# Queries' and keys' parts kept in four slots each, and a head's loads issued as eight transfers of 24 rows

## The reference

```
x = x + attn0(layernorm(x))     # 16 heads of 8 features, causal, with a bias by relative position, then Wo
x = x + ffn0(layernorm(x))      # three tree-routed feed-forward nets give q, k, v of one wide attention
x = x + attn1(layernorm(x))     # 16 heads of 8 features; softmax over all keys, causal mask afterwards
x = x + ffn1(layernorm(x))      # gated, mixed with the token before

# attn0, for a head:                          # attn1, for a head:
sim = q @ k.T + bias;  sim[j > i] = -inf      alpha = softmax(q @ k.T / sqrt(8));  alpha[j > i] = 0
out = softmax(sim) @ v                        out = alpha @ v
```

## Time and profile before

| what | value |
|---|---|
| median of 3 runs | 1780.42 us (1780.28 to 1783.19) |
| the profiled execution | 1783.86 us, of which the span is 1782.1 us |
| open (attn0's projection) | 0 to 65.5 us |
| heads1 (attn0's 64 heads) | 65.5 to about 500 us |
| trees and wide attention | about 500 to 1000 us |
| proj3 (attn1's projection) | about 1000 to 1043 us |
| heads3 (attn1's 64 heads) | 1043 to about 1720 us |
| busy over the span | PE 91%, DVE 85%, ACT 72%, POOL 46% |
| DMA over the span | 141.89 MB, of which loads of heads 512 x 96 KB |

### The profile page before, as it was taken

The page is one execution under the profiler, slowest core; times in us unless marked ns, Lnnn a source line. Parts: engine busy times, 40 slices in busy tenths (PEclk is TensorE's granted clock), DMA queues, the critical chain, the costliest instruction groups (busy, mean ns, idle before and its releaser), DMA issues. The chain is left out here.

```text
span 1782.1 us, 47495 instructions
## 1 busy us (share of the span) xinstructions
PE 1613.3 (91%) x18834; PEld 1038.2 (58%) x18858; DVE 1518.7 (85%) x2248; ACT 1276.2 (72%) x2523; POOL 817.8 (46%) x1533
## 2 busy tenths in 40 slices
PE   5599999999976999999899549999999999999966
PEld 3376667666665887877688314444444444444544
DVE  8699999999856999988677768999999999999735
ACT  6488878888834444454565628888989898998955
POOL 5488888888845001000340323444444444444446
PEclk9699999999965999999999868999999999999978
DMA  7522222323172766565000351111121121112031
GB/s 247 207 85 86 87 90 87 98 86 98 52 148 45 97 95 91 93 90 69 0 1 1 144 184 47 56 56 55 59 65 59 52 73 51 60 53 71 26 76 48
DMA packets 119910, 141.89 MB, mean 80 GB/s; under 512 B 22221, under 2 KB 80778, under 8 KB 119690
## 3 DMA queue, kind: packets, MB, share of 16 engines
q1 hardware_dynamic: 119258, 138.79, 30.8%
q10 hardware_dynamic: 432, 0.07, 0.0%
HBM read 92.70 MB, written 44.98 MB: 77 GB/s over the span
## 5 line engine op out<-in xcount | busy, mean ns | idle before, releaser
L888 DVE TENSOR_REDUCE heads_mx<-heads_psM 128x1 f32<-128x1024 f32 x512 | 602.1, 1219 | 48.4 <-PE heads_psM L979 32.2
L959 ACT ACTIVATE heads_probs<-heads_psS 128x512 f32<-128x512 f32 x1024 | 546.1, 601 | 77.7 <-PE heads_psS L1002 71.7
L928 POOL TENSOR_TENSOR heads_masked<-heads_probs,g_tri 128x128 f32<-128x128 f32 x512 | 233.7, 456 | 360.8 <-ACT heads_probs L959 360.7
L654 POOL TENSOR_TENSOR heads_probs<-heads_probs,one_ebias 128x256 f32<-128x256 f32 (+1 forms) x512 | 341.6, 689 | 76.8 <-ACT heads_probs L686 76.1
L615 DVE TENSOR_REDUCE heads_mx<-heads_psM 128x1 f32<-128x1024 f32 (+7 forms) x512 | 348.8, 748 | 23.7 <-PE heads_psM L697 23.0
L686 ACT ACTIVATE heads_probs<-heads_psS 128x512 f32<-128x512 f32 x576 | 316.3, 603 | 67.6 <-PE heads_psS L697 62.4
L979 PE MATMUL heads_psM<-three_kS,three_qS 48*128 48x512 bf16 x1024 | 230.4, 395 | 20.5 <-PEq L2050 11.6
L1002 PE MATMUL heads_psS<-three_qS,three_kS 50*128 50x512 bf16 x1024 | 238.0, 389 | 0.7 <-ACT heads_probs L959 0.3
L1510 ACT ACTIVATE trees_hid_hi<-trees_hid 128x512 fp32r<-128x512 f32 x192 | 121.6, 633 | 152.4 <-DVE trees_hid L1531 151.5
L1531 DVE SCALAR_TENSOR_TENSOR trees_hid<-trees_psH,g_b,trees_chosen 128x512 f32<-128x512 f32 x192 | 143.8, 749 | 31.8 <-DMA trees_chosen<-leaf_choice 15.1
L1027 PE MATMUL heads_psO<-heads_probs,heads_ones_only 128*32 128x128 f32 x1920 | 162.0, 284 | 0.0
(11 more groups left out here) (273 smaller groups left out, 3174.3 us busy)
## 6 DMA issues: line engine op xcount, KB each, us to landing
trees_chosen<-leaf_choice SPq DMA_DIRECT2D x96, 256.0 KB, 7.6
head_outputs<-g_small SPq DMA_DIRECT2D x128, 128.0 KB
one_qS<-q_parts SPq DMA_DIRECT2D x128, 96.0 KB
one_kS<-k_parts SPq DMA_DIRECT2D x128, 96.0 KB
three_qS<-q_parts SPq DMA_DIRECT2D x128, 96.0 KB
three_kS<-k_parts SPq DMA_DIRECT2D x128, 96.0 KB
q_parts<-g_w SPq DMA_DIRECT2D x8, 768.0 KB, 4.6
k_parts<-g_w SPq DMA_DIRECT2D x8, 768.0 KB, 5.8
```

Source lines behind the costliest of these rows:

```text
L654: pool.tensor_tensor(pr[:, a:a + w], pr[:, a:a + w], bass.AP(eb.tensor, eb.offset + NEAR - 1, [list(eb.ap[0]), [-1, w]]), ALU.mult).then_i ...
L888: dve.tensor_reduce(mx[:, n % 2, k:k + 1], psM[k % 2][:, :], AXX, ALU.max, negate=True).then_inc(max_taken, 1)
L928: pool.tensor_tensor(masked[n % 2][:, kb, :], probs[n % 2][:, kb, kb * P:(kb + 1) * P], g["tri"][:, 0:P], ALU.mult).then_inc(near_done, 1)
L959: act.activation(probs[n % 2][:, kb, h * CH:(h + 1) * CH], ring.bank(i)[:, :], ACT.Exp).then_inc(slot_taken, 1)
```

## The change

The parts are kept in DRAM in four slots, not six (`KEPT`): for queries high, high, middle, low; for keys low, middle, high, high. A tile's 48 rows are now two runs of three neighbouring slots: q takes slots 0 to 2 and then 1 to 3 (high, high, middle, then high, middle, low), k takes 1 to 3 and then 0 to 2 (middle, high, high, then low, middle, high). These are the same six products in another order. Each run is a transfer of its own, of 24 rows, so `Handed.load` issues eight transfers for a head, all on the same semaphore, and what waits for them waits for 128 counts. A store of the high part writes two slots, the others one, so a batch is 8 x 128 rows, 2 MB.

```diff
+KEPT = PARTS + 1
+Q_KEPT = [(0, 2), (2, 1), (3, 1)]
+K_KEPT = [(2, 2), (1, 1), (0, 1)]
...
-                at = b * (PAIRS * P * T)
-                for i, (dst, (start, step, count)) in enumerate(((g["q_dram"], Q_PAIRS[part]), (g["k_dram"], K_PAIRS[part]))):
+                at = b * (KEPT * P * T)
+                for i, (dst, (start, count)) in enumerate(((g["q_dram"], Q_KEPT[part]), (g["k_dram"], K_KEPT[part]))):
                     src = hand.parts[u][:, i, part, :]
-                    sp.dma_start(bass.AP(dst.tensor, at + start * P * T, [[T, P], [step * P * T, count], [1, T]]),
+                    sp.dma_start(bass.AP(dst.tensor, at + start * P * T, [[T, P], [P * T, count], [1, T]]),
                                  bass.AP(src.tensor, src.offset, [list(src.ap[0]), [0, count], [1, T]])).then_inc(stored[u], 16)
...
-        at = (n // HEADS) * PAIRS * P * T + (n % HEADS) * HD * T
-        for tile, src in ((self.qS[u], self.g["q_dram"]), (self.kS[u], self.g["k_dram"])):
+        at = (n // HEADS) * KEPT * P * T + (n % HEADS) * HD * T
+        for tile, src, first in ((self.qS[u], self.g["q_dram"], (0, 1)), (self.kS[u], self.g["k_dram"], (1, 0))):
             for r in (0, HALF):
-                sp.dma_start(tile[r:r + PROWS, :], bass.AP(src.tensor, at, [[P * T, PAIRS], [T, HD], [1, T]])).then_inc(self.loaded[u], 16)
+                for i in range(2):
+                    sp.dma_start(tile[r + i * PARTS * HD:r + (i + 1) * PARTS * HD, :],
+                                 bass.AP(src.tensor, at + first[i] * P * T, [[P * T, PARTS], [T, HD], [1, T]])).then_inc(self.loaded[u], 16)
...
-                    pe.wait_ge(s_loaded[u], (n // BUFS + 1) * 64)
+                    pe.wait_ge(s_loaded[u], (n // BUFS + 1) * 128)
```

More of the change, by code:

```diff
@@ L63 @@
 ROWS = "rows"
-Q_PAIRS = [(0, 1, 3), (3, 1, 2), (5, 1, 1)]
-K_PAIRS = [(1, 2, 3), (0, 4, 2), (2, 1, 1)]
+KEPT = PARTS + 1
+Q_KEPT = [(0, 2), (2, 1), (3, 1)]
+K_KEPT = [(2, 2), (1, 1), (0, 1)]
 KHALF = TPB // 2
@@ L2040, in build @@
             "tri": gm.sb("tri", [P, NEAR]), "masks": gm.sb("masks", [P, 2, 3, P], BF16),
-            "q_dram": nc.dram_tensor("q_parts", [B, PAIRS, P, T], BF16, kind="Internal").ap(),
-            "k_dram": nc.dram_tensor("k_parts", [B, PAIRS, P, T], BF16, kind="Internal").ap(),
+            "q_dram": nc.dram_tensor("q_parts", [B, KEPT, P, T], BF16, kind="Internal").ap(),
+            "k_dram": nc.dram_tensor("k_parts", [B, KEPT, P, T], BF16, kind="Internal").ap(),
             "o_dram": nc.dram_tensor("head_outputs", [B, HEADS, VW, T], F32, kind="Internal").ap(),
```

## The result

The changed kernel takes 1907.81 us (median of 4 runs, 1907.22 to 1909.51) against 1780.35 us before: a ratio of 1.071, 95% interval 1.070 to 1.073. It is 127 us slower. Forecast were +94 us and a range up to 1898: the direction and the place were right, the size was not. Both signs of being wrong that the prediction named came true: SP still waits for ScalarE in heads1, and the round there is 8.51 us, over 8.3. The span of the profiled execution grows by 124.0 us, 1782.1 to 1906.1.

What follows compares the result with a forecast made beforehand. SP (about 80% occupied), TensorE and the loop through load_r were taken as close limits, with SP becoming slowest. Heads1's rounds +83, its start +7, barriers +2 and +2 gave +94 us: 1874 us, 8-in-10 range 1836 to 1898.

Steps and rivals of the forecast that it cites:

- Both signs of being wrong: In heads1, forecast wrong if SP still waits for ScalarE, or if the round is under 7.3 or over 8.3 us.
- SP's price: SP's issuing in heads1: 0.67 us a 24-row load, 0.04 us between two, making SP's round 7.9 us.
- heads3: Rounds stay at 10 us: TensorE's 100% hides the eight loads, so nothing is added.
- The start of heads1 and the barriers: Start of heads1 +7 us; barrier at the end of the opening +2; same barrier at proj3 and heads3 +2.
- the two cases of the prediction: First barrier, end of the opening: 0 to +1 us if bytes hold SP, +5.7 if each store holds it 1.26 us.
- Both fit under 7.9: In heads1, the engines carrying all (7.0 us) and the loop through load_r (7.3 us) stay below SP's 7.9 us round.
- The loop through `mrow`: In heads1, 3.27 us from landing to issue plus up to 4.0 us from issue to landing: 7.3 us.
- SP's wait: SP's wait for ScalarE's mrow in heads1 goes; TensorE instead waits about 1.6 us a head for mrow.
- The clock: Rival: idle TensorE falls to 1.2 GHz in heads1, 8.64 us a round, 1917 us; 13% together with the full-queues case.
- the case in which full queues hold SP up: Rival: full queues hold SP in heads1, about 8.5 us a round, 1908 us; 13% together with the clock rival.
- the rings, not SP: Rival: issuing is cheap; three engines or the loop set heads1's round, 7.0 to 7.3 us; 1828 us, 15%.

Runs made afterwards that it cites:

- eight engines: Changed kernel with the 8 features outermost in each 24-row load's source pattern, so loads use eight DMA engines instead of three: 1858.66 us, ratio 1.042.
- a steady clock: Changed kernel with ten extra matmuls a head in attn0 on TensorE, before it waits for mrow, results overwritten: 1887.25 us, ratio 1.058.
- both together: Changed kernel with the features outermost in the 24-row loads (eight DMA engines) and the ten extra matmuls a head in attn0: 1858.04 us, ratio 1.042.

## Why the prediction was wrong

- *SP's price* was right: forecast 0.67 us and 0.04 between transfers, measured 0.67 (to 0.74 for some) and 0.04. SP's own round is 7.82 us, forecast 7.9. That no engine had the 2.8 us to give was right, as was heads3 (9.97 us, nothing added).
- *The start of heads1 and the barriers* came out right in their sums (+8.2 us with the first barrier, forecast +9), partly by luck. The first round was to stay at 8.64 us and took 7.74, and the next two took 3.2 us more than before where 1.9 were forecast. At the first barrier SP came to its stores 4.9 us later and won 3.1 back on them: its last ten took 1.0 us each where they took 1.3. That is +1.8 us, between the two cases of the prediction, in which +2 was a choice.
- *The failed step* is "Both fit under 7.9". The loop through `mrow` was put at 3.27 + 4.0 = 7.3 us. It is 4.3 + 3.27 = 7.6 at full clock, up to 8.4 with the latest landings (5.15), and 9.0 to 9.5 at low clock, where landing to copy is 4.69. That SP's wait "goes" failed with it: SP waits 26 times in the 57 rounds, 34.6 us, and that is the miss, since without them the rounds would be 4 us under the forecast. The sum allowed for the output directly ahead of `mrow`. With SP without a gap the last loads are always close ahead of it too, and a round that SP alone would end at 7.8 is ended by whichever is later.
- *The clock* was a rival with its whole price, 8.64 us in every round, and had been argued away by one stretch of the opening with a low share at 1.00. It did fall, but for stretches: 0.90 in the mean. The stretch of the opening was no evidence for heads1. A rival that is partly true in every second round wasn't among the cases, nor one in which two of them need each other. Why it falls in about every second round wasn't tried.
- *The 1908 us* of the case in which full queues hold SP up were met by luck: that case has the mean round right (8.5 us), but SP isn't held up, a load still takes it 0.67 us.
- *What each is worth* in heads1's 114 us: with eight engines and a steady clock 66 us are left, which is the issuing. Of the other 48, about 18 are the dearer issuing of loads on three engines (57 x 0.31), and 30 go with SP's waits for `mrow`, 34.6 us in the changed kernel. A steady clock alone leaves 8.5 us of these waits, eight engines alone 4.1, both together none. Taking one away takes most of the other's effect with it, so the late landing and the low clock have no separate prices.
- *The rival "the rings, not SP"* was rejected as a limit of 7.0 us a round, rightly as to the rate. That the same queue acts by latency, long before it is full, was seen as 1 us of landing. With the loads on eight engines SP's waits for `mrow` are 4.1 us, with a steady clock 8.5, with neither edit 34.6: neither cause is the larger part of the miss, the two together are.

## What to carry to other kernels

Price a transfer by three things: what its issuing costs the queue, how many DMA engines its pattern's outermost count gives it, and which small transfer on a short loop stands behind it. When two chains of nearly the same length meet once a round, don't take the longer one: a round ends with whichever is late this time (gapless 7.82 us here, 8.51 in the mean). And an engine that starts to wait may also get slower, as TensorE did.

## What was not expected of the hardware

Reordering the two outer dimensions of a load's source pattern, with the same bytes and the same rows of 2 KB, made a kernel 0.5% faster (before) and about 2.6% faster (changed). A load on eight engines mostly costs SP 0.64 to 0.69 us to issue, on three 0.67, on six 0.68 to 0.75. TensorE's clock fell in heads1 although TensorE was busy 82% of the time there (263.9 of 320 us), and ten matmuls a head whose result nobody reads brought 21 us.
